# Layer-0 attention: scores as two accumulating 64-row products issued beside the maxima products, and maxima of one head's whole row

## The chip, the cores and the metric

One Trainium2 chip, one of its cores. The kernel is one program that runs on that core in a single launch. The metric is the device time of a launch in microseconds (us); lower is better. The engines are named as the profile names them: PE (TensorE), PEld (its weight loads), DVE (VectorE), ACT (ScalarE), POOL (GpSimd), SP (SyncE, which here only issues DMAs).

## What is computed

Two residual layers over x of shape (4, 1024, 128) in float32. The change lies in the attention of the first:

```python
b, n, d = z.shape                       # 4, 1024, 128; 16 heads of 8
qkv = zn @ w_qkv
scores = jnp.einsum('bhqd,bhkd->bhqk', q, k) / SCALING
att = jax.nn.softmax(scores, axis=-1)
out = jnp.einsum('bhal,bhlv->bhav', att, v)
```

All 64 pairs of batch and head need the full 1024 by 1024 score matrix, its maximum over the keys for each query, the exponential and the product with V. Around it stand a layer norm, a gated feed-forward part (computed in the stage before the attention), and in the second layer a landmark attention and a mixture of experts; none of these is touched.

## The kernel before, in words

**Stages.** `layer0_inputs` computes norms, q, k, v and the gate, and stores q and k to DRAM as bf16 parts. `layer0_attention` is the stage that the change rewrites. Everything after it (`layer0_outputs` and the second layer) is left as it is.

**Operands.** A float32 number is held as three bf16 parts. The product of q and k is the sum over 9 pairs of parts, each 8 deep: 72 contraction rows (`ROWS`). Three more rows (`XROWS` = 75) hold minus the maximum of each query in three bf16 parts on the q side and ones on the k side, so that the score leaves TensorE with its maximum already subtracted. Tiles `b_q` and `b_k` hold the 75 rows for 4 heads (a quad); there are 3 slots of them. The maxima need less precision and use only the first 64 rows (`MROWS`). The odd heads have a second copy of these 64 rows in partitions 64 to 127 (`b_qo`, `b_ko`), so that an even and an odd head can be multiplied at once in the two halves of the array.

**Order of the work.** The heads go in 32 duos (2 heads each), a duo in 8 groups (one per block of 128 keys, `kb`), 256 groups in all. All orders are written out by hand in the engines' programs. A group on TensorE, from line 716 on:

- four scores of 128 keys by 512 queries (line 725, key block stationary, 75 rows), numbered n, into PSUM bank 5 + n % 3. Score n waits until exponential n - 3 has read that bank. The order is scores 0, 1, 2, then the products with V, then score 3;
- the products with V of the group before (`times_v`, line 701): four float32 products into four strips of 32 columns, accumulating over the 8 groups of a duo in bank 4 (8 records in the profile);
- two items of the maxima, or three. An item (`maxima_scores`, lines 556 and 557) is two products at once, 64 rows each, for one block of 128 queries and 512 keys of both heads of a later duo, into a pair of banks (0 and 1, or 2 and 3). VectorE takes one maximum for each head from the pair (line 612, 128x1024 to 128x2). An item waits until the pair used two items earlier has been read.

The maxima run ahead of the scores: 25 items (24 of maxima and one transposition) are issued before group 0, the first five of them in `layer0_inputs` (`first_maxima`, `first_maximum`). Once in a duo the 16 maxima per query are folded (line 615) and transposed on TensorE (line 687, an item of its own in the ring of two pairs), VectorE makes minus the maximum and its rest (lines 621 and 623), POOL the second and third part (lines 740 and 742), and SP stores the three parts into the rows of `b_q` (`store_maxima`, line 799, three DMAs). TensorE waits for these DMAs before the first score of a duo.

ScalarE takes the exponential of each score bank into a ring of 12 (line 670) and once per duo copies bank 4 out (`evacuate`, line 662). SP stores that (`store_values`) and loads the next quads (`load_quad`, line 534, 13 DMAs each). In the last duo there are no maxima left; the output projection of batch 0 (`project_piece`, line 190) goes in its place.

Of the kernel before, what the change touches and what calls it, by code (L numbers as in the profile page):

```python
# [5 lines left out]
F32 = mybir.dt.float32  # L6
BF16 = mybir.dt.bfloat16
# [5 lines left out]
P = 128  # L13
B, T, D, H, HD = 4, 1024, 128, 16, 8
NT = B * T // P
TB = T // P
# [4 lines left out]
KROWS = 96  # L21
XROWS = ROWS + NPART
# [146 lines left out]
ITEMS = MAXES + 1  # L169
LATE = 2  # L170
T_GROUP = 5
LEAD = ITEMS + LATE - 2 * T_GROUP
# [10 lines left out]
LOADS0 = 16 * (4 * NPART + 1)  # L183
# [11 lines left out]
def layer0_inputs(g):  # L195
# [4 lines left out]
    g.q0 = [keep(f"b_q{c}", [KROWS, HQ, T], BF16) for c in range(SLOTS)]  # L200
    g.k0 = [keep(f"b_k{c}", [KROWS, HQ, T], BF16) for c in range(SLOTS)]
    g.qo = [keep(f"b_qo{c}", [P, HQ // 2, T], BF16) for c in range(SLOTS)]
    g.ko = [keep(f"b_ko{c}", [P, HQ // 2, T], BF16) for c in range(SLOTS)]
# [3 lines left out]
    g.mx = keep("b_mx", [P, 2, 2, TB, 2])  # L207
# [22 lines left out]
    with nc.Block() as block:  # L230

        @block.vector
        def _(dve):
# [37 lines left out]
            def first_maximum(n):  # L271
                dve.wait_ge(sem("b_max_scores"), n + 1)
                pair = g.bank(2 * (n % 2), 2).rearrange("p (h x) -> p h x", h=2)
                nc.vector.reduce_max(g.mx[:, 0, :, n // 2, n % 2], pair, AX.X).then_inc(sem("b_max_done"), 1)
# [56 lines left out]
        def _(pool):  # L331
# [15 lines left out]
            for b in range(B):  # L347
# [7 lines left out]
                if b == 1:  # L355
                    pool.wait_ge(sem("a_r28"), 2)
                    for c in range(SLOTS):
                        nc.gpsimd.memset(g.k0[c][64:KROWS, :, :].rearrange("p h t -> p (h t)").bitcast(F32),
                                         1.0 + 0x3F80 / 2 ** 23).then_inc(sem("b_ones"), 1)
                        pool.wait_ge(sem("b_ones"), c + 1)  # L360
# [48 lines left out]
        def _(pe):  # L409
# [16 lines left out]
            def first_maxima(lo, hi):  # L426

                for n in range(lo, hi):
                    if n >= 2:
                        pe.wait_ge(sem("b_max_done"), n - 1)  # L430
                    maxima_scores(g, g.q0[0], g.k0[0], g.qo[0], g.ko[0], n, 0, n).then_inc(sem("b_max_scores"), 1)
# [49 lines left out]
        def _(sp):  # L481
# [21 lines left out]
            for b in range(B):  # L503
# [13 lines left out]
                if b == 1:  # L517
                    wait_for_parts(g, sp, 0)
                    sp.wait_ge(sem("b_ones"), SLOTS)
                    load_quad(g, sp, 0, 0)  # L520
# [10 lines left out]
def load_quad(g, sp, quad, c, parts=range(NPART + 1)):  # L531
# [4 lines left out]
    for m in parts:  # L536
# [6 lines left out]
        moved(g.q0[c][lo:lo + NPART * HD, :, :], g.q_ops[quad, :, :, :, :].rearrange(flat))  # L543
        moved(g.k0[c][lo:lo + NPART * HD, :, :], g.k_ops[quad, :, m:m + NPART, :, :].rearrange(flat))
        odd = slice(MROWS + lo, MROWS + lo + n * HD)
        moved(g.qo[c][odd, :, :], g.q_ops[quad, 1:HQ:2, 0:n, :, :].rearrange(flat))
        moved(g.ko[c][odd, :, :], g.k_ops[quad, 1:HQ:2, m:m + n, :, :].rearrange(flat))
# [12 lines left out]
def max_items():  # L560

    seq = []
    for d in range(DUOS):
        for i in range(MAXES):
            if i == LATE and d:
                seq.append((d - 1, None))
            seq.append((d, i))
    return seq + [(DUOS - 1, None)]


def layer0_attention(g):
# [7 lines left out]
    with ExitStack() as mem:  # L579
# [3 lines left out]
        m = sb("b_m", [P, 2, MAXES])  # L583
# [10 lines left out]
    q, k, v, qo, ko, mx = g.q0, g.k0, g.v0, g.qo, g.ko, g.mx  # L594
# [3 lines left out]
    AV = g.bank(4)  # L598
    seq = max_items()
    through = lambda kb: 2 * (kb + 1) + (kb >= T_GROUP)  # L600
    upto = lambda d, kb: min(len(seq), ITEMS * (d + 1) - 1 + LEAD + through(kb))

    with nc.Block() as block:

        @block.vector
        def _(dve):
            def item(n):
                d, i = seq[n]
                dve.wait_ge(sem("b_max_scores"), n + 1)
                if i is not None:  # L610
                    pair = g.bank(2 * (n % 2), 2).rearrange("p (h x) -> p h x", h=2)
                    nc.vector.reduce_max(mx[:, d % 2, :, i // 2, i % 2], pair, AX.X).then_inc(sem("b_max_done"), 1)  # L612
                    if i == MAXES - 1:
                        dve.wait_ge(sem("b_max_done"), n + 1)
                        nc.vector.reduce_max(m[:, d % 2, :], mx[:, d % 2, :, :, :].rearrange("p h t a -> p (h t) a"),
                                             AX.X).then_inc(sem("b_m"), 1)
                    return
                mT = g.bank(2 * (n % 2))[0:MAXES, 0:P]
                if d:
                    dve.wait_ge(sem("b_m_loaded"), 16 * NPART * d)  # L620
                nc.vector.tensor_scalar(neg[:, 0, :], mT, -1.0, None, ALU.mult).then_inc(sem("b_first"), 1)
                dve.wait_ge(sem("b_first"), d + 1)
                nc.vector.scalar_tensor_tensor(neg_rest[:, :], mT, -1.0, neg[:, 0, :], ALU.mult, ALU.subtract)\  # L623
                  .then_inc(sem("b_max_done"), 1)

            for n in range(FIRST, upto(0, -1)):
                item(n)
            for d in range(DUOS):
                for n in range(upto(d, -1), upto(d, TB - 1)):
                    item(n)  # L630
# [26 lines left out]
        def _(act):  # L657
# [5 lines left out]

            for d in range(DUOS):
                for u in range(4 * TB):
                    n = 4 * TB * d + u
                    act.wait_ge(sem("b_scores"), n + 1)
                    if n >= E_RING:
                        act.wait_ge(sem("b_av"), (n - E_RING) // 4 + 1)
                    act.activation(ex[:, n % E_RING, :], g.bank(5 + n % 3), ACT.Exp, scale=ATT_SCALE)\  # L670
# [6 lines left out]
        def _(pe):  # L677
            def item(n):
                d, i = seq[n]
                s, p = d // 2 % SLOTS, d % 2  # L680
                if i == 0 and p == 0 and d:
                    pe.wait_ge(sem(f"b_loaded{s}"), LOADS0 * (d // 2 // SLOTS + 1))
                if n >= 2:
                    pe.wait_ge(sem("b_max_done"), n - 1)
                if i is None:
                    pe.wait_ge(sem("b_m"), d + 1)
                    nc.tensor.transpose(g.bank(2 * (n % 2))[0:MAXES, 0:P], m[:, d % 2, :], g.ident[:, :])\
                      .then_inc(sem("b_max_scores"), 1)
                    return
                maxima_scores(g, q[s], k[s], qo[s], ko[s], n, p, i).then_inc(sem("b_max_scores"), 1)  # L690

            def times_v(group):
# [6 lines left out]
                for i in range(4):  # L699
                    at_v = (2 * p + i // 2) * P + kb * 2 * HD  # L700
# [4 lines left out]
            def project_piece(piece):  # L705
                if piece == 0:
                    pe.wait_ge(sem("b_max_done"), len(seq))
                    pe.wait_ge(sem("d_oT"), 1)
# [4 lines left out]
            for n in range(FIRST, upto(0, -1)):  # L713
                item(n)
            for d in range(DUOS):
                s, p = d // 2 % SLOTS, d % 2
# [1284 lines left out]
```

## Time and profile before

| | |
|---|---|
| median of 3 runs | 1371.28 us (1370.59 to 1373.99) |
| profiled execution: span | 1372.0 us |
| profiled execution: mean granted TensorE clock | 0.952 of full speed |
| attention stage in it | first score at 115.96 us, last product with V starts at 811.56 us |
| busy in the span | PE 91%, DVE 74%, ACT 62%, POOL 17% |

The profiled execution's span lies 0.7 us above the median and inside the runs' range. "Busy" of PE is modelled: a 512-column product is shown for 0.39 us from its start at the full clock, while the next one may start after 0.21 us, so starts are to be compared, not ends. Where two products stand with the same start, they run at once in the two halves of the array. All instructions of one kind that follow each other directly are merged into one row of the timeline with their count.

### The profile page before, as it was taken

Reading aid. Unit: us, or ns where it says so; the run is one execution under the profiler, and the core shown is the slowest. Engines: PE = TensorE matmul, PEld = TensorE weight load, DVE = VectorE, ACT = ScalarE, POOL = GpSimd, SP = SyncE. Lnnn points to the kernel's source line nnn. Section 1 sums busy time; section 2 is a strip of 40 time slices with the busy share of each in tenths; the row PEclk is TensorE's granted clock in tenths of the full one; section 3 lists DMA queues with packets and bytes.
Section 4 is the critical chain, followed back from the end, with each engine's and each line's share of the span. In section 5 each row is a group of like instructions: output and inputs, shape, how many; then the busy total and the mean of one; then the engine's idle time right before and its main releaser. Section 6 shows DMA issues by size and latency. Waiting matters only on the chain. (4 is left out here: it accounts for less than half of the span.)

```text
span 1372.0 us, 25967 instructions
## 1 busy us (share of the span) xinstructions
PE 1249.1 (91%) x10305; PEld 580.1 (42%) x10305; DVE 1009.4 (74%) x1288; ACT 851.8 (62%) x1447; POOL 237.5 (17%) x309
## 2 busy tenths in 40 slices
PE   6968999999999999999999978998899899899980
PEld 4631222222222222222222225555699566688870
DVE  6878898998899989998999737665676588623324
ACT  3533888888888888888888866555421366533431
POOL 4200110000000000000000002000385222135560
PEclk9986999999999999999999989998999599999995
DMA  5763033232323313222231121100011111123316
GB/s 147 202 199 79 26 65 64 50 76 45 74 64 82 76 40 78 51 66 66 50 74 40 69 71 48 47 16 16 17 31 39 55 44 36 46 69 102 100 58 188
DMA packets 75204, 94.96 MB, mean 69 GB/s; under 512 B 13236, under 2 KB 44684, under 8 KB 74052
## 3 DMA queue, kind: packets, MB, share of 16 engines
q1 hardware_dynamic: 69996, 83.19, 23.9%
q0 software_dynamic: 5088, 10.12, 2.4%
q8 instruction: 81, 1.33, 0.4%
q14 instruction: 39, 0.32, 0.1%
HBM read 54.30 MB, written 38.56 MB: 68 GB/s over the span
## 5 line engine op out<-in xcount | busy, mean ns | idle before, releaser
L670 ACT ACTIVATE b_exp_ring<-psum 128x512 f32<-128x512 f32 x1024 | 555.6, 600 | 148.8 <-PE psum L725 145.6
L612 DVE TENSOR_REDUCE b_mx<-psum 128x2 f32<-128x1024 f32 x507 | 595.8, 1218 | 66.5 <-PE psum L557 65.4
L725 PE MATMUL psum<-b_q,b_k 75*128 75x512 bf16 x1024 | 312.4, 387 | 1.5 <-ACT b_exp_ring L670 1.5
L701 PE MATMUL psum<-b_exp_ring,b_v 128*32 128x512 f32 x2048 | 274.5, 608 | 0.9 <-ACT b_exp_ring L670 0.7
L725 PEld LDWEIGHTS psum<-b_q,b_k 75*128 75x128 bf16 x1024 | 79.3, 97 | 317.0 <-ACT b_exp_ring L670 221.8
L556 PE MATMUL psum<-b_k,b_q 64*128 64x512 bf16 x512 | 168.9, 395 | 25.5 <-DVE b_mx L612 10.6
L557 PE MATMUL psum<-b_ko,b_qo 64*128 64x512 bf16 x512 | 168.9, 395 | 0.0
L740 POOL CAST b_neg<-b_neg_rest 16x128 bf16<-16x128 f32 x32 | 8.9, 279 | 639.6 <-DVE b_neg_rest L623 639.6
L1834 ACT ACTIVATE e_hT<-psum,e_b 128x358 f32<-128x358 f32 (+3 forms) x96 | 53.6, 559 | 75.4 <-PE psum L1854 72.0
L556 PEld LDWEIGHTS psum<-b_k,b_q 64*128 64x128 bf16 x512 | 44.7, 93 | 128.6 <-DVE b_mx L612 41.4
L701 PEld LDWEIGHTS psum<-b_exp_ring,b_v 128*32 128x32 f32 x2048 | 41.3, 108 | 108.6 <-issue 106.0
L1764 POOL DMA_INDIRECT y_tok<-e_y,e_dest x72 | 70.8, 984 | 70.7 <-DVE e_y L1806 51.5
L1274 POOL DMA_INDIRECT x_disp<-x_norm,row_sent x64 | 63.3, 989 | 91.3 <-PE psum L1632 81.3
L1864 PE MATMUL psum<-e_w,e_hT 128*128 128x128 f32 (+1 forms) x576 | 67.4, 277 | 0.0
L1864 PEld LDWEIGHTS psum<-e_w,e_hT 128*128 128x128 f32 (+1 forms) x576 | 64.6, 184 | 1.8
L1612 ACT ACTIVATE f_le<-f_lx 128x1024 f32<-128x1024 f32 x32 | 33.8, 1057 | 47.4 <-DVE f_lx L1574 47.4
L1000 DVE TENSOR_REDUCE c_nm<-psum 128x1 f32<-128x1024 f32 x32 | 37.7, 1220 | 32.2 <-PE psum L1157 32.1
L1854 PE MATMUL psum<-e_xT,e_w 128*128 128x358 f32 (+3 forms) x192 | 60.2, 468 | 0.9 <-DVE e_xT L1778 0.9
L1568 DVE TENSOR_REDUCE f_max<-psum 128x16 f32<-128x1024 f32 x32 | 39.2, 1224 | 24.4 <-PE psum L1632 23.5
L1104 ACT ACTIVATE c_en<-psum,c_nm 128x1024 f32<-128x1024 f32 x32 | 35.7, 1116 | 32.8 <-DVE c_nm L1000 32.8
L1450 PE MATMUL psum<-i_x,i_az 64*64 64x64 f32 x1536 | 47.0, 218 | 1.6 <-DVE i_x L1381 1.5
L1182 PE MATMUL psum<-ident,c_en 128*128 128x128 f32 x256 | 36.7, 289 | 12.2 <-ACT c_en L1104 8.4
(278 smaller groups left out, 1427.6 us busy)
## 6 DMA issues: line engine op xcount, KB each, us to landing
b_q<-q_ops SPq DMA_DIRECT2D x48, 192.0 KB
b_k<-k_ops SPq DMA_DIRECT2D x48, 192.0 KB
k_ops<-a_k SPq DMA_DIRECT2D x20, 256.0 KB, 3.3
x_disp<-b_zeros SPq DMA_DIRECT2D x13, 320.0 KB
e_x<-x_disp SPq DMA_DIRECT2D x8, 520.0 KB
v_ops<-a_vs SPq DMA_DIRECT2D x4, 1024.0 KB, 5.1
b_v<-v_ops SPq DMA_DIRECT2D x16, 256.0 KB
av_out<-b_acc SPq DMA_DIRECT2D x128, 32.0 KB, 1.7
```

Of the source, the lines that this page charges most:

```text
L556: g.nc.tensor.matmul(g.bank(2 * (n % 2)), q[0:MROWS, 2 * p, t], k[0:MROWS, 2 * p, keys], start=True, stop=True)
L557: return g.nc.tensor.matmul(g.bank(2 * (n % 2) + 1), qo[MROWS:P, p, t], ko[MROWS:P, p, keys], start=True, stop=True)
L612: nc.vector.reduce_max(mx[:, d % 2, :, i // 2, i % 2], pair, AX.X).then_inc(sem("b_max_done"), 1)
L670: act.activation(ex[:, n % E_RING, :], g.bank(5 + n % 3), ACT.Exp, scale=ATT_SCALE)\
L701: last = nc.tensor.matmul(AV[32 * i:32 * i + 32, :], v[s][:, at_v:at_v + 32], ex[:, (4 * group + i) % E_RING, :], start=(kb == 0), stop=(k ...
L725: nc.tensor.matmul(g.bank(5 + n % 3), k[s][0:XROWS, h, kb * P:(kb + 1) * P], q[s][0:XROWS, h, half * BANK:(half + 1) * BANK], start=True, ...
L1274: pool.indirect_dma_start(g.x_disp[:, :], bass.IndirectOffsetOnAxis(g.rows_out[:, n:n + 1], 0), g.XNW[:, n % NT, :], None).then_inc(g.sem( ...
L1450: last = nc.tensor.matmul(out[half, i, :], lhs(n * GR + i, half), rhs(n * GR + i, half), start=True, stop=True)
L1764: pool.indirect_dma_start(g.y_tok[:, :], bass.IndirectOffsetOnAxis(dest[c][0:r, t:t + 1], 0), y[c][0:r, t, :], None).then_inc(sem(f"e_sent ...
L1834: act.activation(hT[c][:, i, lo:hi], g.ps[:, (3 + n % 3) * BANK:(3 + n % 3) * BANK + hi - lo], ACT.Gelu, bias=b1[c][:, i:i + 1]).then_inc( ...
L1854: nc.tensor.matmul(g.ps[:, (3 + n % 3) * BANK:(3 + n % 3) * BANK + hi - lo], w1[c][:, i * P:(i + 1) * P], xT[:, lo:hi], start=True, stop=T ...
L1864: last = nc.tensor.matmul(g.ps[0:r, col:col + D], hT[c][:, i, t * P:t * P + r], w2[c][:, i, :], start=(i == 0), stop=(i == HC - 1))
```

## The change

- Scores: each score is now two products of 64 rows that accumulate in the same bank: the first with 64 of the 72 part rows (`main_scores`, tiles `b_q`, `b_k`), the second (`rest_scores`, tiles `b_qr`, `b_kr`) with the remaining 8 rows, the 3 rows of the maxima, and 53 rows that are zero on the q side. Even heads lie in partitions 0 to 63 and odd heads in 64 to 127, for the scores and the maxima alike, so the second copy for the maxima goes.
- Order: in a group the scores alternate between an even and an odd head (i % 2 is the head, i // 2 the half of the queries). Maxima products of one head are issued beside score products of the other. The products with V come last in the group.
- Maxima: an item is one head and one block of 128 queries with all 1024 keys: two products in the same half of the array into the two banks of a unit, one maximum per query (128x1024 to 128x1). There are two items per group, 24 before group 0 (`LEAD` = 12 groups). The fold over halves (line 615) goes.
- Minus the maximum: the transposed maxima are negated by ScalarE (`negated`), and POOL makes all three parts (cast, subtract, cast, subtract). The transposition stands at the end of group 4 of the duo before (`turned`). SP stores six pieces in place of three.
- Loads: a quad takes 17 DMAs in place of 13, of fewer bytes (8 of the 72 rows once each in place of the second copy).

The core of the diff:

```diff
-def maxima_scores(g, q, k, qo, ko, n, p, i):
-
-    t, keys = slice(i // 2 * P, i // 2 * P + P), slice(i % 2 * BANK, i % 2 * BANK + BANK)
-    g.nc.tensor.matmul(g.bank(2 * (n % 2)), q[0:MROWS, 2 * p, t], k[0:MROWS, 2 * p, keys], start=True, stop=True)
-    return g.nc.tensor.matmul(g.bank(2 * (n % 2) + 1), qo[MROWS:P, p, t], ko[MROWS:P, p, keys], start=True, stop=True)
+def head_rows(odd):
+
+    return slice(MROWS * odd, MROWS * odd + MROWS)
+
+def maxima_scores(g, c, x, j, half, n):
+
+    rows, p, t = head_rows(1 - j), x // TB % 2, x % TB
+    return g.nc.tensor.matmul(g.bank(2 * (n % M_RING) + half), g.q0[c][rows, p, t * P:(t + 1) * P],
+                              g.k0[c][rows, p, half * BANK:(half + 1) * BANK], start=True, stop=True)
...
+            def maxima(x, which=range(2)):
+                for j in which:
+                    n = place[x, j]
+                    dve.wait_ge(sem("b_max_scores"), n + 1)
+                    nc.vector.reduce_max(maximum_of(mx, x, j), g.bank(2 * (n % M_RING), 2), AX.X)\
+                      .then_inc(sem("b_max_done"), 1)
...
+            def negated(d):
+                act.wait_ge(sem("b_max_scores"), place[d, None] + 1)
+                if d:
+                    act.wait_ge(sem("b_third"), d)
+                act.activation(neg_all[:, :], g.bank(2 * (place[d, None] % M_RING))[0:MAXES, 0:P], ACT.Copy, scale=-1.0)\
+                   .then_inc(sem("b_neg_all"), 1)
...
+            def turned(d):
+                n = place[d, None]
+                pe.wait_ge(sem("b_max_done"), MAXES * (d + 1))
+                until_free(pe, n)
+                nc.tensor.transpose(g.bank(2 * (n % M_RING))[0:MAXES, 0:P],
+                                    mx[:, d % 2, :, :].rearrange("p h t -> p (h t)"), g.ident[:, :])\
+                  .then_inc(sem("b_max_scores"), 1)
+
+            def main_scores(group, i):
+
+                d, kb = group // TB, group % TB
+                s, p, rows, n = d // 2 % SLOTS, d % 2, head_rows(i % 2), 4 * group + i
+                if n >= S_RING:
+                    pe.wait_ge(sem("b_exp_done"), n - S_RING + 1)
+                nc.tensor.matmul(S_BANK(n), k[s][rows, p, kb * P:(kb + 1) * P],
+                                 q[s][rows, p, i // 2 * BANK:(i // 2 + 1) * BANK], start=True, stop=False)
+
+            def rest_scores(group, i):
+
+                d, kb = group // TB, group % TB
+                s, p, rows = d // 2 % SLOTS, d % 2, head_rows(i % 2)
+                if kb == 0 and i == 0:
+                    pe.wait_ge(sem("b_m_loaded"), 16 * 2 * NPART * (d + 1))
+                nc.tensor.matmul(S_BANK(4 * group + i), kr[s][rows, p, kb * P:(kb + 1) * P],
+                                 qr[s][rows, p, i // 2 * BANK:(i // 2 + 1) * BANK], start=False, stop=True)\
+                  .then_inc(sem("b_scores"), 1)
...
+            for group in range(TB * DUOS):
+                d, kb, x = group // TB, group % TB, group + LEAD
+                more = x < SETS
+                if d == DUOS - 1 and kb in PROJECT_AT:
+                    project_piece(PROJECT_AT.index(kb))
+                main_scores(group, 0)
+                if more:
+                    maxima(x, 0, 0)
+                rest_scores(group, 0)
+                if more:
+                    maxima(x, 0, 1)
+                main_scores(group, 1)
+                main_scores(group, 2)
+                rest_scores(group, 1)
+                rest_scores(group, 2)
+                if more:
+                    maxima(x, 1, 0)
+                main_scores(group, 3)
+                if more:
+                    maxima(x, 1, 1)
+                rest_scores(group, 3)
+                if group:
+                    times_v(group - 1)
+                if turned_in(group) is not None and turned_in(group) < DUOS:
+                    turned(turned_in(group))
             times_v(TB * DUOS - 1)
...
             def parts(d):
-                pool.wait_ge(sem("b_max_done"), seq.index((d, None)) + 1)
+                pool.wait_ge(sem("b_neg_all"), d + 1)
+                if d:
+                    pool.wait_ge(sem("b_m_loaded"), 16 * 2 * NPART * d)
+                nc.gpsimd.tensor_copy(neg[:, 0, :], neg_all[:, :]).then_inc(sem("b_first"), 1)
+                pool.wait_ge(sem("b_first"), d + 1)
+                nc.gpsimd.tensor_tensor(neg_rest[:, :], neg_all[:, :], neg[:, 0, :], ALU.subtract)\
+                      .then_inc(sem("b_rest"), 1)
+                pool.wait_ge(sem("b_rest"), d + 1)
...
                 for i in range(NPART):
+                    sp.wait_ge(sem(("b_first", "b_second", "b_third")[i]), d + 1)
+                    for odd in range(2):
+                        row = MROWS * odd + HD + i
+                        dst = qr[d // 2 % SLOTS][row:row + 1, d % 2, :]
+                        sp.dma_start(dst.rearrange("r (t x) -> r t x", x=P), neg[TB * odd:TB * (odd + 1), i, :])\
+                          .then_inc(sem("b_m_loaded"), 16)
```

Here `x` counts sets of two items (one block of 128 queries, both heads), `S_RING` is 3 and `M_RING` 2. `until_free(eng, n)` waits for the read of the item two places earlier: VectorE's maximum, or ScalarE's copy where that item was a transposition. `turned_in(group)` gives a duo at every eighth group (4, 12, 20 and so on).

## Rows read from the trace of the kernel before

**Rows 1.** The page, busy time of each engine in the whole span.

```profile
PE 1249.1 (91%) x10305; PEld 580.1 (42%) x10305; DVE 1009.4 (74%) x1288; ACT 851.8 (62%) x1447; POOL 237.5 (17%) x309
```

**Rows 2.** Windows view: busy us of each engine (instructions), granted clock, DMA share, GB/s.

```profile
96.00:108.00 12.00, 6.47 (x22) 1.14 (x22) 11.97 (x13) 0.00 (x0) 0.00 (x0) 0.50 0.77 154
116.00:128.00 12.00, 12.00 (x42) 1.92 (x40) 6.36 (x7) 6.38 (x12) 0.00 (x0) 0.51 0.65 129
128.00:780.00 652.00, 641.80 (x3879) 156.36 (x3881) 589.08 (x575) 533.28 (x992) 33.98 (x72) 1.00 0.26 61
```

**Rows 3.** Timeline of PE, a steady group and a transposition: start, duration, count.

```profile
499.68 0.82 PE L725 MATMUL psum<-b_q,b_k 75*128 75x512 bf16 x3
500.43 1.07 PE L701 MATMUL psum<-b_exp_ring,b_v 128*32 128x512 f32 x8
501.43 0.39 PE L725 MATMUL psum<-b_q,b_k 75*128 75x512 bf16 x1
501.75 0.39 PE L556 MATMUL psum<-b_k,b_q 64*128 64x512 bf16 x1
...
501.99 0.39 PE L556 MATMUL psum<-b_k,b_q 64*128 64x512 bf16 x1
...
502.31 0.82 PE L725 MATMUL psum<-b_q,b_k 75*128 75x512 bf16 x3
...
504.29 0.28 PE L687 MATMUL psum<-ident,b_m 128*16 128x128 f32 x1
504.60 0.39 PE L556 MATMUL psum<-b_k,b_q 64*128 64x512 bf16 x1
```

**Rows 4.** Timeline of DVE, maxima ahead of the groups and in a steady group.

```profile
95.01 12.54 DVE L612 TENSOR_REDUCE b_mx<-psum 128x2 f32<-128x1024 f32 x11 [1.12 <-PE psum L557]
...
510.68 2.36 DVE L612 TENSOR_REDUCE b_mx<-psum 128x2 f32<-128x1024 f32 x2 [0.25 <-PE psum L557]
```

**Rows 5.** Timeline of PE, the last groups, which have no maxima.

```profile
781.74 0.82 PE L725 MATMUL psum<-b_q,b_k 75*128 75x512 bf16 x3
...
786.21 0.82 PE L725 MATMUL psum<-b_q,b_k 75*128 75x512 bf16 x3
787.28 0.39 PE L725 MATMUL psum<-b_q,b_k 75*128 75x512 bf16 x1 [0.26 <-ACT b_exp_ring L670]
787.61 1.06 PE L701 MATMUL psum<-b_exp_ring,b_v 128*32 128x512 f32 x8
788.60 0.82 PE L725 MATMUL psum<-b_q,b_k 75*128 75x512 bf16 x3
...
791.23 0.61 PE L190 MATMUL psum<-wproj,d_oT 128*128 128x128 f32 x4
791.67 0.81 PE L725 MATMUL psum<-b_q,b_k 75*128 75x512 bf16 x3
...
811.56 1.06 PE L701 MATMUL psum<-b_exp_ring,b_v 128*32 128x512 f32 x8 [0.69 <-ACT b_exp_ring L670]
```

**Rows 6.** Timeline of ACT, the exponentials of the same groups.

```profile
786.63 2.06 ACT L670 ACTIVATE b_exp_ring<-psum 128x512 f32<-128x512 f32 x4 [0.17 <-PE psum L725]
```

**Rows 7.** Source view, lines 670 and 725: duration ns min/median/max, first and last start.

```profile
L670 ACT ACTIVATE b_exp_ring<-psum x1024: 592/597/632, 116.6 to 810.9; 128x512 f32<-128x512 f32 x171
...
L725 PEld LDWEIGHTS psum<-b_q,b_k x1024: 95/97/152, 116.0 to 810.5; 75*128 75x128 bf16 x171
```

**Rows 8.** Timeline of PE, from the first scores to the full clock.

```profile
115.96 1.91 PE L725 MATMUL psum<-b_q,b_k 75*128 75x512 bf16 x4
...
128.12 0.82 PE L725 MATMUL psum<-b_q,b_k 75*128 75x512 bf16 x3
```

**Rows 9.** Tile view of b_neg and timeline of SP: steps and DMAs of minus the maximum.

```profile
L742 POOL TENSOR_TENSOR b_neg<-b_neg_rest,b_neg x32: 415/416/418, 111.0 to 785.8; 16x128 bf16<-16x128 f32 x32
...
DMA to landing us min/median/max: 1.6/1.7/3.6
...
505.22 1.78 SPq L799 DMA_DIRECT2D b_q<-b_neg  x3
```

More of the change, by code:

```diff
@@ L597, in layer0_attention, with until_free @@
     tiles = lambda ap: ap.rearrange("p (n c) -> p n c", c=P)
-    AV = g.bank(4)
+    AV = g.bank(2 * M_RING)
+    S_BANK = lambda n: g.bank(2 * M_RING + 1 + n % S_RING)
     seq = max_items()
-    through = lambda kb: 2 * (kb + 1) + (kb >= T_GROUP)
-    upto = lambda d, kb: min(len(seq), ITEMS * (d + 1) - 1 + LEAD + through(kb))
+    place = {item: n for n, item in enumerate(seq)}
+    turned_in = lambda group: (group + LEAD) // TB - 1 if (group + LEAD) % TB == 0 else None
+    def until_free(eng, n):
+        if n >= M_RING:
+            before, j = seq[n - M_RING]
+            if j is None:
+                eng.wait_ge(sem("b_neg_all"), before + 1)
+            else:
+                eng.wait_ge(sem("b_max_done"), 2 * before + j + 1)
     with nc.Block() as block:
@@ L606, in _ @@
         def _(dve):
[L607 to L627, printed above, removed]
+            def maxima(x, which=range(2)):
[3 more added lines that the diff above has]
+                    nc.vector.reduce_max(maximum_of(mx, x, j), g.bank(2 * (n % M_RING), 2), AX.X)\
+                      .then_inc(sem("b_max_done"), 1)
+            maxima(FIRST // 2, range(FIRST % 2, 2))
+            for x in range(FIRST // 2 + 1, LEAD):
+                maxima(x)
             for d in range(DUOS):
-                for n in range(upto(d, -1), upto(d, TB - 1)):
-                    item(n)
+                for x in range(TB * d + LEAD, min(TB * (d + 1) + LEAD, SETS)):
+                    maxima(x)
                 b = d // 8 - 1
@@ L666, in _ @@
                     n = 4 * TB * d + u
+                    if u % 4 == 0 and n and turned_in(n // 4 - 1) is not None and turned_in(n // 4 - 1) < DUOS:
+                        negated(turned_in(n // 4 - 1))
                     act.wait_ge(sem("b_scores"), n + 1)
@@ L677, in _, with maxima @@
         def _(pe):
[L678 to L690, printed above, removed]
+            def maxima(x, j, half):
+                n, d = place[x, j], x // TB
+                if d and d % 2 == 0 and x % TB == 0 and j == 0 and half == 0:
+                    pe.wait_ge(sem(f"b_loaded{d // 2 % SLOTS}"), LOADS0 * (d // 2 // SLOTS + 1))
+                if half == 0:
+                    until_free(pe, n)
+                last = maxima_scores(g, d // 2 % SLOTS, x, j, half, n)
+                if half == 1:
+                    last.then_inc(sem("b_max_scores"), 1)
@@ L712, in _ @@
             pe.wait_ge(sem("b_rows_set"), SLOTS)
[L713 to L716, printed above, removed]
[L717 to L731 removed]
+            for n in range(FIRST, 2 * LEAD):
+                for half in range(2):
+                    maxima(n // 2, n % 2, half)
+                if n % 2 and turned_in(n // 2 - LEAD) == 0:
+                    turned(0)
```

104 lines of the change are left out of this document (44 added, 60 removed).

## The prediction, made before the changed kernel was built

> **What bounds the kernel now.** I read the page's busy times first, then the windows of the attention stage, then single groups in the timelines of PE, DVE and ACT. PE has the largest share of the whole span [rows 1]. That is an average over stages, so the stage decides. From 128 to 780 us PE is busy 641.80 of 652.00 us, DVE 589.08 and ACT 533.28, at the full clock of 2.4 GHz [rows 2]. In one group of the timeline [rows 3] the reader is to see that PE never waits. Three scores start 0.215 apart (three in 0.82 us, one being shown as 0.39); after the third the products with V start (500.43, so 0.32 after it); 1.00 later comes score 3; 0.32 later the first pair of maxima products, 0.24 later the second, 0.32 later the next group. The sum is 2.63 us. DVE needs 2.36 us for two maxima [rows 4], and less in a stream: 11 in 12.54 us against 2 in 2.36 gives (12.54 - 2.36) / 9 = 1.13 each, 2.26 for two. ACT takes four exponentials in 2.06 us [rows 6], of which one lasts 0.60 [rows 7], so they start 0.49 apart. So a group is bound by PE's order of work, with DVE 0.3 us behind it. From group 3 (128.12) [rows 8] to group 244 (781.74) [rows 5] 241 groups take 653.6 us, 2.712 each. That is 2.63 and, once per 8 groups, about 0.66 for the transposition and what it delays.
>
> The last twelve groups have no maxima, and they show what matters most below [rows 5, 6]. There PE does wait. The score that starts at 786.21 is ready for ACT at 786.63 (0.42), its exponential runs 0.60 to 787.23, and the score that needs that bank starts at 787.28 (0.05). The products with V start at 787.61 (0.33) and the next scores at 788.60 (0.99). This ring of waits is 2.39 us long and sets the pace of the tail.
>
> **PE's products, part by part.** Before, a group has four 75-row scores and two pairs, six places in all; after, twelve 64-row products, issued so that even and odd heads alternate: six pairs. A pair costs 0.235 (0.24 above) [rows 3] if both halves run at once, as the maxima do now. The switches between scores and maxima go: 0.32 against 0.215, twice, about 0.2 us per group. PE's own chain is then five steps of 0.235, 0.33 to the products with V, and 0.99 back: 2.50 us.
>
> The Trainium skill (TensorEngine Tiling (Array Packing), Key Properties) says that changing the tiling mode drains the array. Here that is the 0.1 us at each switch, so the trace agrees; by this rule alone a group would go to 2.50 us and the kernel would gain, the first rival below.
>
> **The wait that this exposes.** Score 3 uses the bank of score 0 and must wait for exponential 0. Now 1.75 us lie between the starts of scores 0 and 3, since the products with V are between them (0.75 + 1.00) [rows 3]. After, only four pair steps do, 0.94 us. What must fit in: the second product of score 0 starts 0.235 later, ready 0.42 after that, exponential 0.60, release 0.05: 1.305 us. So PE stands 0.365 us before the first product of score 3 in every group. Behind it in PE's queue stand the last maxima product, the products with V, and the next group's score 0, which starts the same ring again. It is the ring of the tail with two doubled scores in it: 2.39 + 2 x 0.23 = 2.85 us per group. The ends: 0.215 for a doubled step and no drain before the V products gain 0.07 (2.78); 0.26 and a dearer switch from 64-row products to the V strips lose 0.09 (2.94). I take 2.85, as all its terms have rows.
>
> **Who else could be later.** DVE: its first item is ready at 0.235 + 0.42 = 0.66 after the group's start, the second at 1.305 + 0.42 = 1.73. It finishes at about 3.0, 0.1 us into the next group, where its bank is wanted only 0.94 into it. It is idle 0.5 us per group. ACT has 1.95 us of work in 2.85. Neither sets the pace. Reading one head's 1024 keys is the same 128x1024 read as two heads' 512, so I leave its duration at 1.22.
>
> **The transposition.** It moves after the V products. Today it takes 0.31 of PE (504.29 to 504.60) [rows 3], then two DVE steps hold its pair of banks. After, the copy is ACT's, which is idle then, and the pair is wanted again only 0.94 into the next group. I take 0.3 per duo, with ends of 0.1 (nothing but its stream) and 0.7 (as today). The fold on DVE (line 615) and the two DVE steps were hidden or inside that 0.66.
>
> **Minus the maximum.** From the transposition (0.28 us [rows 3]) on: ACT's copy, at most the 0.60 of an exponential [rows 7]; POOL's steps at most 0.42 each with 0.08 between [rows 9]; six DMAs of 0.59 (three in 1.78), the first after POOL's first step. The last is issued at 0.3 + 0.6 + 0.4 + 3.6 = 4.9 us and lands 1.7 later [rows 9], at 6.6. The second product of the next duo's score 0 wants it three groups and 0.23 us after the transposition: 8.8 us. Slack 2.2 us, none if it lands like the worst, 3.6. I cost it at nothing. SP issues four more loads per quad and three more of these DMAs per duo. Each issue is about half a us, SP serves two duos (45 us) with one quad, and nothing behind it is due within several groups.
>
> **Ahead of the groups.** In `layer0_inputs` and in the lead an item's two products now follow each other in one half. At the half clock (0.50 [rows 2]) that makes an item ready 0.43 us later. A pair of banks now goes round in 1.22 (read) + 0.05 (release) + 0.64 (product to reader: first score 115.96 [rows 8], first exponential 116.6 [rows 7]) = 1.91 us, against two reads in 2.26. With 0.43 more it is 2.34, so 0.08 per round of two: about +1 us over the lead's ten rounds, and I take +0.5 for the five items in the inputs (ends 0 and 5 x 0.43). The first three groups run at the half clock and take 12.2 us [rows 8], PE without a gap [rows 2]. The new order costs about the same there. A clock that rises in the lead, where PE will stream twice as long, would save up to 12.2 - 3 x 2.85 = 3.6 us. I take 0.
>
> **The sum,** against the profiled execution:
> - lead and inputs +1.5;
> - groups 3 to 243: 241 x 2.85 + 30 x 0.3 = 695.9 against 653.6, so +42.2;
> - groups 244 to 255: 12 x 2.82 (both products of a score at 0.215), the four pieces of the projection, which lie in the ring now (0.44 each, 791.23 to 791.67 [rows 5]), 0.3 for the last transposition, and 1.06 for the last V products: 37.0 against 812.62 - 781.74 = 30.9, so +6.1. DVE's chain after the projection stays hidden;
> - later stages start later by the sum: 0.
>
> Together +49.8 us. The profiled span (1372.0) lies 0.7 above the median of the runs; against the median that makes 1371.3 + 49.8 = 1421.
>
> **Rivals.**
> - *Faster, the wait does not bite* (10%). If score 0's exponential is back within 0.94 us, PE's chain of 2.50 sets the pace: 241 x 2.50 + 9 = 611 against 653.6, and +3 elsewhere: 1332 us. For it: two switches fewer, no DVE steps held. Against: 0.42 + 0.60 + 0.05 stands in the rows of the tail. The point of decision is a group of (653.6 - 9) / 241 = 2.67: the wait of 0.365 would have to halve.
> - *No change* (3%): the two just cancel, 1371.
> - *Minus the maximum lands late* (5%). Its place is the second product of a duo's first score. Each us beyond the slack of 2.2 costs 31: at one us, 1452.
> - *Weight loads no longer hide* (5%). Each product now follows another in the same rows. If its load of 0.097 us [rows 7] were paid, a step is 0.31 and the ring 3.01: 253 x 0.16 = 40 more, 1461. Against: the three scores at 0.215 have such loads in the same rows, and pay nothing [rows 3].
> - *The halves do not run at once* where accumulating products are in play (3%): 11 x 0.215 + 0.33 + 0.99 = 3.69 per group, about 1625.
>
> On the fourth: the Trainium skill (TensorE: Matmul & The Clock Gate, Part 3) says that a weight load overlaps running products only where the row group differs. That would be its mechanism here; the steps of 0.215 between the scores of before speak against it.
>
> **How the numbers follow.** The forecast, 1421, has 74%, with a range of its own from 1399 (2.78 per group and the early clock) to 1446 (2.94). To hold 8 in 10 the range takes in most of the late landing as well: 1398 to 1456. About 0.3% (4 us) is what a measurement of this kernel can tell from no change. Faster by more: 10%; within it: 3%; slower by more: 87%.
>
> **What would show it.** In the changed timeline: groups 2.85 us apart; the first product of score 3 about 1.3 us after that of score 0, released by ACT; V products 0.56 after it; the next group 0.99 later. ACT waits about 0.8 us per group for PE, above all at exponential 0. DVE waits about 0.5. A group of 2.50 with ACT and DVE nearly without waits would prove me wrong on the ring. Pair steps over 0.25 would speak for the weight loads, and a PE wait for the DMA of b_neg once per duo for the late landing.

## The result and the profile after

The changed kernel takes 1407.6 us (median of 4 runs, 1407.45 to 1409.95) against 1370.93 us for the kernel before on the same chip (1368.39 to 1373.99). The ratio is 1.0271, with a 95% interval of 1.0252 to 1.0289: 2.7% slower. The prediction was 1421 us with a range of 1398 to 1456, so the direction and the range held, and the loss was over-estimated: 37 us measured, 50 forecast.

From the page of the changed kernel, the busy times of a span of 1408.2 us, and the costliest groups of the attention (busy us, mean ns, then the idle time before them and who ended it):

```profile
PE 1289.2 (92%) x11329; PEld 592.4 (42%) x11329; DVE 988.3 (70%) x1192; ACT 837.7 (59%) x1479; POOL 260.2 (18%) x376
...
L633 DVE TENSOR_REDUCE b_mx<-psum 128x1 f32<-128x1024 f32 x507 | 596.8, 1218 | 118.9 <-PE psum L563 118.7
L691 ACT ACTIVATE b_exp_ring<-psum 128x512 f32<-128x512 f32 x1024 | 528.9, 603 | 163.6 <-PE psum L732 163.4
...
L723 PEld LDWEIGHTS psum<-b_q,b_k 64*128 64x128 bf16 x1024 | 74.2, 93 | 356.5 <-ACT b_exp_ring L691 323.3
```

Next to [rows 1], every engine's share is about the same or lower (PE and POOL a point higher). No engine has become clearly fuller; the stage has become longer. ACT waits 163.4 us for scores where it waited 145.6 in the kernel before (page, line 670), DVE 118.7 us for maxima where it waited 65.4 (line 612), and PE's weight loads of the first product wait 323.3 us for exponentials. That last sum alone proves nothing: the loads of the scores waited 221.8 us before too (line 725), although PE lost no time in a steady group. The windows view shows the stage:

```profile
96.00:108.00 12.00, 9.55 (x22) 1.15 (x18) 11.38 (x10) 0.00 (x0) 1.19 (x1) 0.50 0.53 120
...
128.00:780.00 652.00, 642.49 (x4611) 160.62 (x4609) 542.29 (x462) 494.80 (x973) 53.48 (x128) 1.00 0.18 47
```

From 128 to 780 us DVE is now busy 542 us in place of 589 and ACT 495 in place of 533 [rows 2], while PE is shown busy 642 of 652 as before. That figure misleads here: a 512-column product is shown for 0.39 us, so a product that starts 0.41 after the one before it leaves almost no idle time. The starts in PE's timeline show it. One steady group (only the second maxima product of the last pair, at 502.16, is left out; the row 502.69 is the products with V):

```profile
500.86 0.39 PE L723 MATMUL psum<-b_q,b_k 64*128 64x512 bf16 x1
500.87 0.39 PE L563 MATMUL psum<-b_k,b_q 64*128 64x512 bf16 x1
501.09 0.38 PE L732 MATMUL psum<-b_qr,b_kr 64*128 64x512 bf16 x1
501.09 0.38 PE L563 MATMUL psum<-b_k,b_q 64*128 64x512 bf16 x1
501.30 0.38 PE L723 MATMUL psum<-b_q,b_k 64*128 64x512 bf16 x2
501.52 0.38 PE L732 MATMUL psum<-b_qr,b_kr 64*128 64x512 bf16 x2
501.74 0.38 PE L563 MATMUL psum<-b_k,b_q 64*128 64x512 bf16 x1
502.15 0.39 PE L723 MATMUL psum<-b_q,b_k 64*128 64x512 bf16 x1
...
502.38 0.38 PE L732 MATMUL psum<-b_qr,b_kr 64*128 64x512 bf16 x1
502.69 1.07 PE L745 MATMUL psum<-b_exp_ring,b_v 128*32 128x512 f32 x8
503.68 0.39 PE L723 MATMUL psum<-b_q,b_k 64*128 64x512 bf16 x1
```

What to see, against [rows 3]: the six steps are there. At 500.86 and 501.09 a score's product and a maxima product of the other head start together, then two products of scores, each step 0.215 to 0.23 long. The maxima product due at 501.74 is in place too. The first product of score 3 would be due beside it, and starts at 502.15, 0.41 later and 1.29 after the first product of score 0. Then 0.54 to the V products, and 0.99 to the next group: 2.82 us. ACT and DVE in the same group:

```profile
501.50 2.06 ACT L691 ACTIVATE b_exp_ring<-psum 128x512 f32<-128x512 f32 x4 [0.76 <-PE psum L732]
```

```profile
501.54 2.36 DVE L633 TENSOR_REDUCE b_mx<-psum 128x1 f32<-128x1024 f32 x2 [0.44 <-PE psum L563]
```

Score 0 is ready for ACT at 501.50 (0.64 after its first product). Its exponential of 0.60 ends at 502.10, and PE starts score 3 at 502.15. This is the ring of waits that the tail of before showed [rows 5, 6], with a doubled score in front and one behind. DVE waits 0.44 to 0.47 per group, ACT 0.76.

The start of the stage and the first transposition, on PE:

```profile
118.67 0.63 PE L723 MATMUL psum<-b_q,b_k 64*128 64x512 bf16 x1
...
127.71 0.39 PE L723 MATMUL psum<-b_q,b_k 64*128 64x512 bf16 x1
...
133.35 0.28 PE L713 MATMUL psum<-ident,b_mx 128*16 128x128 f32 x1
133.56 0.39 PE L723 MATMUL psum<-b_q,b_k 64*128 64x512 bf16 x1
```

The last groups have no maxima and yet the same pace: from V products to V products 3.03 us where a transposition of 0.21 lies between (815.75 to 818.78), then 2.83 (to 821.61). So the maxima have no part in it:

```profile
813.93 0.39 PE L723 MATMUL psum<-b_q,b_k 64*128 64x512 bf16 x2
...
815.75 1.06 PE L745 MATMUL psum<-b_exp_ring,b_v 128*32 128x512 f32 x8
...
818.78 1.06 PE L745 MATMUL psum<-b_exp_ring,b_v 128*32 128x512 f32 x8
...
821.61 1.06 PE L745 MATMUL psum<-b_exp_ring,b_v 128*32 128x512 f32 x8
```

### The profile page after: what moved, and what is told of

The parts are those of the page before. It is cut to its first block and busy times, and to the rows that moved or that the text cites. A ratio compares the mean times of both kernels' runs of the same rounds, so it can differ in the third digit from the quotient of the medians.

```text
span 1408.2 us, 28176 instructions
## 1 busy us (share of the span) xinstructions
PE 1289.2 (92%) x11329; PEld 592.4 (42%) x11329; DVE 988.3 (70%) x1192; ACT 837.7 (59%) x1479; POOL 260.2 (18%) x376
## 5 line engine op out<-in xcount | busy, mean ns | idle before, releaser
L633 DVE TENSOR_REDUCE b_mx<-psum 128x1 f32<-128x1024 f32 x507 | 596.8, 1218 | 118.9 <-PE psum L563 118.7
L691 ACT ACTIVATE b_exp_ring<-psum 128x512 f32<-128x512 f32 x1024 | 528.9, 603 | 163.6 <-PE psum L732 163.4
L563 PE MATMUL psum<-b_k,b_q 64*128 64x512 bf16 x1024 | 353.9, 391 | 11.0 <-DVE b_mx L633 4.5
L723 PE MATMUL psum<-b_q,b_k 64*128 64x512 bf16 x1024 | 298.2, 383 | 13.1 <-ACT b_exp_ring L691 3.1
L732 PE MATMUL psum<-b_qr,b_kr 64*128 64x512 bf16 x1024 | 292.8, 377 | 0.0
L723 PEld LDWEIGHTS psum<-b_q,b_k 64*128 64x128 bf16 x1024 | 74.2, 93 | 356.5 <-ACT b_exp_ring L691 323.3
L798 POOL CAST b_neg<-b_neg_all 16x128 bf16<-16x128 f32 x32 | 9.0, 280 | 641.3 <-ACT b_neg_all L679 641.3
L563 PEld LDWEIGHTS psum<-b_k,b_q 64*128 64x128 bf16 x1024 | 75.1, 94 | 54.8 <-DVE b_mx L633 20.4
L732 PEld LDWEIGHTS psum<-b_qr,b_kr 64*128 64x128 bf16 x1024 | 75.6, 95 | 29.0 <-issue 0.4
```

The source lines that it names most:

```text
L563: return g.nc.tensor.matmul(g.bank(2 * (n % M_RING) + half), g.q0[c][rows, p, t * P:(t + 1) * P], g.k0[c][rows, p, half * BANK:(half + 1) ...
L633: nc.vector.reduce_max(maximum_of(mx, x, j), g.bank(2 * (n % M_RING), 2), AX.X)\
L691: act.activation(ex[:, n % E_RING, :], S_BANK(n), ACT.Exp, scale=ATT_SCALE)\
L723: nc.tensor.matmul(S_BANK(n), k[s][rows, p, kb * P:(kb + 1) * P], q[s][rows, p, i // 2 * BANK:(i // 2 + 1) * BANK], start=True, stop=False)
L732: nc.tensor.matmul(S_BANK(4 * group + i), kr[s][rows, p, kb * P:(kb + 1) * P], qr[s][rows, p, i // 2 * BANK:(i // 2 + 1) * BANK], start=Fa ...
```

## Experiments

**1. The V products back before score 3.**

```diff
@@ group loop of the changed kernel
                 rest_scores(group, 2)
+                if group:
+                    times_v(group - 1)
                 if more:
                     maxima(x, 1, 0)
                 main_scores(group, 3)
...
                 rest_scores(group, 3)
-                if group:
-                    times_v(group - 1)
```

> The products with V go back to their old place, after the scores 0 to 2 and before score 3. Theory (ring of three banks): of any four scores between two V products the first and the last share a bank, so the wait does not go, it moves to score 2 (which needs exponential 3 of the group before). A group stays 2.82 us, the kernel at 1407 us (within 6). Rival (the place of the V products alone exposes the exponential, as score 3 was covered by them before): a group of 2.50 us, about 1327 us.

Measured: 1443.79 us (1443.27 to 1444.32), ratio to before 1.054 (1.0509 to 1.057). Neither number was right, but the rival is out: nothing was gained. PE, two steady groups and the group with a transposition:

```profile
401.57 1.07 PE L745 MATMUL psum<-b_exp_ring,b_v 128*32 128x512 f32 x8
...
402.57 0.39 PE L723 MATMUL psum<-b_q,b_k 64*128 64x512 bf16 x1
...
403.44 0.84 PE L723 MATMUL psum<-b_q,b_k 64*128 64x512 bf16 x2
...
404.42 1.07 PE L745 MATMUL psum<-b_exp_ring,b_v 128*32 128x512 f32 x8
...
418.81 1.07 PE L745 MATMUL psum<-b_exp_ring,b_v 128*32 128x512 f32 x8
...
420.35 0.28 PE L713 MATMUL psum<-ident,b_mx 128*16 128x128 f32 x1
...
421.73 0.39 PE L563 MATMUL psum<-b_k,b_q 64*128 64x512 bf16 x1 [0.79 <-DVE b_mx L633]
...
422.69 1.06 PE L745 MATMUL psum<-b_exp_ring,b_v 128*32 128x512 f32 x8
```

The V products come 2.85 to 2.86 apart in a steady group. The row 403.44 holds the first products of scores 1 and 2; it lasts 0.84, not the 0.60 of two that follow each other, because score 2 now waits there. So the wait moved from score 3 to score 2, as the theory has it, and the ring is 0.04 longer (in ACT's timeline the exponential of score 3 starts at 403.24, 0.67 after its first product, and not 0.64; why, I did not find out). What I had not foreseen is the group with the transposition (420.35): from V products to V products it takes 3.88 us. There the transposition follows almost directly on the group's last maxima product, and the next item's bank is still being read by DVE, so PE waits 0.79 for it. That is 1.02 us per duo more than a steady group, against 0.21 when the V products lie in between. Over 31 duos the difference makes 25 us, and 0.04 in each of some 220 steady groups another 9: 34 of the 36 us.

**2. The V products of two groups together.**

```diff
-                if group:
-                    times_v(group - 1)
+                if group and group % 2 == 0:
+                    times_v(group - 2)
+                    times_v(group - 1)
...
+            times_v(TB * DUOS - 2)
             times_v(TB * DUOS - 1)
```

> The V products of two groups are done together after every second group. Theory: eight scores lie between them, and the ring's step of 1.29 us (first product of a score to first product of the score three later) counts from score 0 to 3, 3 to 6 and 4 to 7, so score 7 starts 3.0 us after score 0; 0.22 + 0.31 + 0.93 + 1.00 more makes 5.47 us for two groups, 2.73 each: about 1386 us. Rival (V products placed last expose one wait for each time they are done, so half of the 0.32 us goes): 2.66 each, about 1367 us. If PE's own products set the pace: no change but a switch, 1400 us or more.

Measured: 1407.78 us (1406.95 to 1408.6), the time of the changed kernel. PE and ACT over two groups:

```profile
502.72 0.39 PE L723 MATMUL psum<-b_q,b_k 64*128 64x512 bf16 x1
...
504.01 0.39 PE L723 MATMUL psum<-b_q,b_k 64*128 64x512 bf16 x1
...
505.97 0.39 PE L723 MATMUL psum<-b_q,b_k 64*128 64x512 bf16 x1
...
508.36 0.39 PE L723 MATMUL psum<-b_q,b_k 64*128 64x512 bf16 x1
```

```profile
503.36 4.13 ACT L691 ACTIVATE b_exp_ring<-psum 128x512 f32<-128x512 f32 x8 [1.51 <-PE psum L732]
```

Two groups take 5.64 us (502.72 to 508.36), 2.82 each. Score 3 starts 1.29 after score 0, as expected. But score 7 starts at 505.97, 3.25 after score 0, and not 3.0. ACT shows why: its eight exponentials follow each other without a gap (4.13 us), the first five of them 0.48 to 0.49 apart. Score 7's bank is freed by exponential 4, and that one is held by its predecessors, not by its own score: 0.64 + 4 x 0.49 + 0.60 + 0.05 = 3.25. My working had counted the ring from score to score alone. So the ring of three banks holds, with a second side to it: while PE does scores alone, ACT's 0.49 per exponential is the pace, and while PE does V products, ACT runs dry after three banks.

**3. A shorter exponential.**

```diff
-    act.activation(ex[:, n % E_RING, :], S_BANK(n), ACT.Exp, scale=ATT_SCALE)
+    act.activation(ex[:, n % E_RING, 0:BANK // 2], S_BANK(n)[:, 0:BANK // 2], ACT.Exp, scale=ATT_SCALE)
```

POOL also sets the ring to 1.0 once, and ScalarE waits for that before the first exponential.

> The exponential takes only 256 of a bank's 512 columns (the other half of each ring place stays 1.0, so half of the exponentials is left out); PE and DVE do the same work. Theory: the exponential is a link of the ring, so the group shortens by what one exponential shortens, estimated at 0.2 us (0.60 to about 0.4), down to 2.61 us: about 1354 us, with ACT busy far less than before. Rival (weight loads or PE's own 64-row steps set the pace): ACT has slack already, so no change, 1407 us.

Measured: 1358.7 us (1358.59 to 1358.82). PE in one group:

```profile
500.38 0.39 PE L724 MATMUL psum<-b_q,b_k 64*128 64x512 bf16 x1
...
501.46 0.39 PE L724 MATMUL psum<-b_q,b_k 64*128 64x512 bf16 x1
...
502.99 0.39 PE L724 MATMUL psum<-b_q,b_k 64*128 64x512 bf16 x1
```

The group is 2.61 us (500.38 to 502.99), and score 3 starts 1.08 after score 0 in place of 1.29. The exponential itself, in the lines view by form:

```profile
L692 ACT ACTIVATE b_exp_ring<-psum 128x256 f32<-128x256 f32 x986 | 344.6, 383 | 239.2 <-PE psum L733 227.8
```

It takes 0.38 us in place of 0.60, and the group is shorter by the same 0.21. ACT was idle for 0.76 us in each group of the changed kernel, and yet less work on it gave 49 us. Its idle time was no slack: the exponential of score 0 lies on the ring. The rival is out.

**4. One product per score.** The second product of each score, with the remaining 8 rows and the maxima, is left out, and the exponential's scale is smaller.

```diff
-    q[s][rows, p, i // 2 * BANK:(i // 2 + 1) * BANK], start=True, stop=False)
+    q[s][rows, p, i // 2 * BANK:(i // 2 + 1) * BANK], start=True, stop=True).then_inc(sem("b_scores"), 1)
...
-    nc.tensor.matmul(S_BANK(4 * group + i), kr[s][rows, p, kb * P:(kb + 1) * P],
-                     qr[s][rows, p, i // 2 * BANK:(i // 2 + 1) * BANK], start=False, stop=True)\
-      .then_inc(sem("b_scores"), 1)
```

> The second product of each score is left out, and the exponential's scale is made 64 times smaller to keep it finite; all waits stay. Theory: the ring holds two second products (score 0's before its exponential, score 3's before the V products), 0.215 us each, so a group goes from 2.82 to 2.39 us (the period of the tail of before), with DVE's 2.26 us close behind: about 1300 us. Rival (second products are free beside others, and it is the order of V products and waits alone that costs): 2.6 us or more, 1350 us or more.

Measured: 1316.22 us (1315.33 to 1317.11).

```profile
501.36 1.06 PE L743 MATMUL psum<-b_exp_ring,b_v 128*32 128x512 f32 x8
...
503.43 0.39 PE L723 MATMUL psum<-b_q,b_k 64*128 64x512 bf16 x1 [0.23 <-ACT b_exp_ring L691]
...
503.75 0.64 PE L743 MATMUL psum<-b_exp_ring,b_v 128*32 128x512 f32 x4
```

From V products to V products (501.36 to 503.75) it is 2.39 us, as expected and as in the tail of before; the kernel is 16 us above the expectation. Two second products of 0.215 account for 2.82 - 2.39 = 0.43 us. The 16 us are 0.5 per duo. I had no term for the duo's copy of the V bank on ACT and none for DVE, which is nearly full at this pace. The starts of one duo show both. In the group where ACT copies the V bank (480.10 to 480.59, the exponential of score 0 right behind it) the V products come 2.59 after the last ones, 0.20 more than in a steady group. The group with the transposition and the one behind it take 2.62 each: 0.21 of that is the transposition itself, as in the changed kernel, and 0.25 comes from PE waiting for maxima that DVE has not read yet (at 490.39 and 493.44). Together that is 0.45 per duo, 14 of the 16 us.

**5. A fourth bank for the scores.** Eight banks are in use: four for maxima, one for V, three for scores. This version gives the scores four and the maxima three single ones. An item of the maxima is then one head, 128 queries and 512 keys, four per group; DVE reads 512 columns at a time and folds the two halves once per duo.

```diff
-M_RING = 2
-S_RING = 3
+M_RING = 3
+S_RING = 4
...
-    AV = g.bank(2 * M_RING)
-    S_BANK = lambda n: g.bank(2 * M_RING + 1 + n % S_RING)
+    AV = g.bank(4)
+    S_BANK = lambda n: g.bank((3, 5, 6, 7)[n % S_RING])
...
+    rows, p, t, half = head_rows(1 - i % 2), x // TB % 2, x % TB, i // 2
+    return g.nc.tensor.matmul(g.bank(n % M_RING), g.q0[c][rows, p, t * P:(t + 1) * P],
+                              g.k0[c][rows, p, half * BANK:(half + 1) * BANK], start=True, stop=True)
...
                 main_scores(group, 0)
                 if more:
                     maxima(x, 0)
                 rest_scores(group, 0)
                 main_scores(group, 1)
                 if more:
                     maxima(x, 1)
                 rest_scores(group, 1)
                 main_scores(group, 2)
                 if more:
                     maxima(x, 2)
                 rest_scores(group, 2)
                 main_scores(group, 3)
                 if more:
                     maxima(x, 3)
                 rest_scores(group, 3)
                 if group:
                     times_v(group - 1)
```

> A fourth bank for scores (score n waits for exponential n - 4), paid by the maxima: they have three single banks, an item is one head, 128 queries and 512 keys, VectorE takes four maxima of 512 per group and folds once per duo. The V products stay last. Theory (ring of three banks): score 3 has a bank of its own, the wait goes, and PE's chain of 2.50 us sets the pace (five steps of 0.22 to 0.235, 0.31, 1.00), with DVE close behind (four reads of an estimated 0.59 make 2.37): about 1327 us, below both kernels. Rival 1 (weight loads or steps set the pace): 2.8 us or more, 1400 us. Rival 2 (DVE's shorter reads cost more than 0.62 us each): DVE becomes the bound, above 2.5 us and PE waits for it: 1340 us or more.

Measured: 1327.3 us (4 runs, 1326.28 to 1328.78) against 1368.89 for before: ratio 0.9696 (0.9677 to 0.9714). It is 3% faster than the kernel before and 80 us faster than the changed one, in which only the banks, the maxima's items and the order of the products around them differ. PE in one group:

```profile
500.32 0.39 PE L727 MATMUL psum<-b_q,b_k 64*128 64x512 bf16 x1
500.33 0.39 PE L563 MATMUL psum<-b_k,b_q 64*128 64x512 bf16 x1
...
501.20 0.38 PE L727 MATMUL psum<-b_q,b_k 64*128 64x512 bf16 x1
501.50 0.39 PE L563 MATMUL psum<-b_k,b_q 64*128 64x512 bf16 x1
...
501.82 1.06 PE L749 MATMUL psum<-b_exp_ring,b_v 128*32 128x512 f32 x8
502.82 0.39 PE L727 MATMUL psum<-b_q,b_k 64*128 64x512 bf16 x1
```

The group is 2.50 us (500.32 to 502.82). Score 3's first product starts 0.88 after score 0's, with no wait for ACT. The theory of the ring of scores is right: with a bank of its own, score 3 waits for nothing. That the group is then the expected 2.50 is in part luck. I had added up PE's chain from steps of up to 0.235; the measured ones are 0.23 once and 0.215 after that, so five steps, 0.31 and 0.99 make 2.40. The other 0.1 is a wait. PE's last step (501.20 to 501.50) is 0.30 and not 0.215. DVE's read of the group's first item (timeline of DVE, 500.76 to 501.30), and DVE's sums in the lines view of the stage (128 to 740 us):

```profile
500.75 0.69 DVE L634 TENSOR_REDUCE b_mx<-psum 128x1 f32<-128x512 f32 x1
```

```profile
L634 DVE TENSOR_REDUCE b_mx<-psum 128x1 f32<-128x512 f32 x961 | 595.9, 682 | 9.5 <-PE psum L563 6.7
```

The first and the last of a group's four maxima products (500.33 and 501.50) share one of the three banks. The first is ready for DVE 0.42 after its start, DVE reads it until 501.44, and PE starts the last 0.06 later. This 0.06 is the same in each of the 238 groups between 130 and 740 us that show all four products. So a second ring of banks, now that of the maxima, sets the pace of a steady group: 0.42 + 0.69 + 0.06 = 1.17, then 0.32 to the V products and 1.00 to the next group, 2.49. DVE is nearly full (idle for 9.5 us of 612), but its reads start 0.60 apart where none waits for its product, 2.41 for four. This second ring is read from the rows; no run changes one of its links alone.

**6. The same with three banks for the scores.**

Against experiment 5 one line changes:

```diff
 M_RING = 3
-S_RING = 4
+S_RING = 3
```

> As the kernel with four banks, but with three used for the scores (only the ring's length changed back). Theory: the split of the maxima is not what helps, so the ring is back at 2.82 us per group, and the time at 1407 us (within 8). Rival (the gain of four_banks comes from the smaller maxima items and their new places): about as fast as four_banks.

Measured: 1409.45 us (1405.67 to 1413.23).

```profile
500.69 0.39 PE L727 MATMUL psum<-b_q,b_k 64*128 64x512 bf16 x1
...
501.98 0.39 PE L727 MATMUL psum<-b_q,b_k 64*128 64x512 bf16 x1
...
503.51 0.39 PE L727 MATMUL psum<-b_q,b_k 64*128 64x512 bf16 x1
```

The group is 2.82 us again, score 3 again 1.29 after score 0. This one number undoes the whole gain of experiment 5. The smaller items, their places and the fold make no difference of their own while the ring of scores sets the pace.

**7. The kernel before with its V products last.**

```diff
@@ group loop of the kernel before
-                        if i == 2 and d + kb:
-                            times_v(TB * d + kb - 1)
+                    if d + kb:
+                        times_v(TB * d + kb - 1)
                     for n in range(upto(d, kb - 1), upto(d, kb)):
                         item(n)
```

> The kernel before with one edit: the V products of the group before are done after score 3 and not before it. Theory: the four scores then lie between two V products, with no maxima among them, so score 3 waits for exponential 0: 0.42 + 0.60 + 0.05 = 1.07 us from score 0 to score 3, then 0.33 + 1.00 + 0.24 + 0.32 back: 2.96 us in place of 2.63, about 1450 us. Rival (PE's products alone set the pace of before): the same 2.63 us, 1371 us.

Measured: 1453.32 us (1451.82 to 1454.82).

```profile
502.05 0.82 PE L725 MATMUL psum<-b_q,b_k 75*128 75x512 bf16 x3
503.13 0.39 PE L725 MATMUL psum<-b_q,b_k 75*128 75x512 bf16 x1 [0.26 <-ACT b_exp_ring L670]
```

Score 3 (503.13) starts 1.08 after score 0 (502.05), where three scores that follow each other need 0.645. In this kernel's timeline the V products of steady groups are 2.93 to 2.94 apart, against 2.61 to 2.63 before (2.96 was expected). The kernel before thus had the same ring and hid it, in a way that experiment 1 explains: the maxima (0.32 + 0.24 + 0.32 us from score 3 to the next score 0 [rows 3]) stood inside the four scores between two V products. In the changed kernel they run beside the scores and fill no time in it.

## Why the prediction was right, and where its sizes were off

**PE's products.** Right. The halves run at once also with accumulating products, and a step is 0.215 to 0.23. Two of the five rivals (weight loads no longer hide, the halves do not run at once) fall with the rows of the steady group: three steps of 0.215 in the same half (501.09, 501.30, 501.52, 501.74) with a load of 0.093 us each (median in the source view of line 723) are as short as the step of the scores before [rows 3], where a load that is paid would have made them 0.31. The sentence of the Trainium skill that speaks for the first of them (TensorE: Matmul & The Clock Gate, Part 3) is not borne out here. PE's own chain, though, was over-estimated: its steps add up to 2.40 per group and not 2.50.

**The wait.** Right in place and size: score 3's first product 1.29 after score 0's (1.305 forecast), a wait of 0.41 in place of 0.365. Experiments 3, 4 and 6 change one link of the ring each (exponential, second products, number of banks) and the group follows by 0.21, 0.43 and 0.32 us. That the ring sets the pace is shown, not only argued. The bank gives back 0.32 and not the whole 0.41, because the ring of the maxima takes over at 2.50 (experiment 5).

**The term that was mis-sized** is the ring's length: 2.39 + 2 x 0.23 = 2.85. The doubled steps on the ring cost 0.215 each, which the sum itself took for the tail. With 2.82 the term is 7 us smaller. The ends of the range were not worked out cleanly either: two steps of 0.215 give 2.82 and a drain of 0.1 less would give 2.72, where the text has 2.78, and 2.94 leads to 1444 us, where it has 1446. The term-by-term comparison, in us, from the profiled execution of either kernel:

| | forecast | measured |
|---|---|---|
| first score later | +1.5 | +2.7 (118.67 against 115.96) |
| groups 0 to 2 | 0 | -3.1 (127.71 - 118.67 against 12.16) |
| groups 3 to 243 | +42.2 | +32.6 (813.93 - 127.71 against 653.62) |
| of it the ring | 241 x 2.85 | 241 x 2.82, 7.2 less |
| of it 30 transpositions | 0.30 each | 0.22 each, 2.4 less |
| groups 244 to 255 | +6.1 | +6.8 (851.57 - 813.93 against 30.88) |
| later stages | 0 | -2.8 (556.6 against 559.4) |
| sum | +49.8 | +36.2 |

**The clock in the first groups.** I had priced an early rise at up to 3.6 us and taken 0; it gave 3.1. From 96 to 108 us PE is busy 9.55 of 12 us at 0.50 where it had 6.47 [rows 2], and the steps of the products fall from 0.43 to 0.215 us at about 123 us, against 128 before. That the busier lead brought the earlier rise is not tested.

**Later stages.** Their code is unchanged, and their length from the end of the last V product to the end of the span is 559.4 us in the execution of before and 556.6 after; over the profiled executions of all nine kernels it lies between 555.0 (four banks) and 560.0 (three banks, experiment 6). So a difference of some 4 us between two single executions says nothing about the change. I set the prediction against a profiled span of 1372.0 us and called it 0.7 above the median; this execution's own time is 1373.99 us, the slowest of the runs shown, so it stood 2.7 above. A span is some 2 us shorter than the time of its own execution. The difference of the medians, 36.7 us, is the same as that of the spans, 36.2, within this.

**Hidden steps.** DVE and ACT had the slack that was forecast (0.45 and 0.76 us per group). Minus the maximum did not become late: no wait of PE for these DMAs appears among the waits, though the six take 0.635 us each and 4.05 us together (4.18 in the first duo), a little more than the 3.6 I had reckoned.

**The faster rival** (PE's chain of 2.50 sets the pace, 1332 us) did not come about. With the fourth bank the group is 2.50 us and the kernel 1327 us, close to its number, but by luck: PE's own chain is about 2.4 there, and the ring of the maxima holds it at 2.50.

## What to carry to other kernels

When a producer and a consumer go round through a few banks, work out the time from the first to the last item that share one (here 0.64 + 0.60 + 0.05 us) and compare it with what else the producer does in between. Work that is moved out of that stretch, or is made to run beside it, exposes the wait, even though the consumer has no more to do and shows more idle time. The test is to shorten the consumer or to add a bank: if an engine that is idle a quarter of the time still sets the pace, it is a link of such a ring, and a bank taken from a neighbour with slack may be worth more than another order of instructions (here 80 us against none in experiments 1 and 2). Then work out the neighbour's ring too: it may be the next to set the pace.

## What the runs showed that I had not expected

- A transposition placed right behind a maxima item costs 1.02 us per duo instead of 0.21 (experiment 1), through the bank that DVE has not read yet.
- Grouping the V products by two gained nothing (1407.78 us): a chain of exponentials 0.48 to 0.49 us apart takes the place of the second exposed wait.
- VectorE's reads of 512 columns from a single bank start 0.60 us apart in a run, 1.13 for 1024 columns [rows 4]: halving the items costs 2.41 - 2.26 = 0.15 us of DVE per group. With three single banks it also makes a second ring of banks (experiment 5).
